# A decoder's second cross-attention: fillers out of TensorE's score units, and GpSimd's row scaling rewritten

## The reference

```
x = x + xattn(layernorm(x), ctx_2048, ...)   # layernorm: (x - mean) / sqrt(var + 1e-5)
q = (x @ Wq + bq) ;  k, v = split(ctx @ Wkv + bkv)      # 16 heads of 16 features
q, k = int8-like rounding per head ;  v rounded per column
attn = softmax(q @ k.T)                                 # all 1024 queries against all 1024 keys
attn = round(attn / (max / 255)) * (max / 255)          # codes 0 .. 255 per row
out  = (attn @ v) @ Wp + bp
x = x + moe(layernorm(x), ...)
```

## Time and profile before

| | us |
|---|---|
| median of 3 runs | 539.23 (538.76 to 540.14) |
| the profiled execution | 539.08 |
| its span in the trace | 537.3 |
| score units: first score product to end of last exponential | 223.12 to 406.2 |
| PE busy | 426.8 (79%) |
| DVE busy | 417.2 (78%) |
| ACT busy | 339.0 (63%) |
| POOL busy | 260.9 (49%) |

### The profile page before, as it was taken

One profiled execution on the slowest core, in us unless ns is written; L12 is line 12 of the kernel. 1 busy time (PEld: TensorE's weight loads), 2 busy tenths in 40 slices (PEclk: granted clock), 3 DMA queues, 4 the chain that ended last, 5 costly groups with the idle time before them and its releaser, 6 DMA issues.

```text
span 537.3 us, 11046 instructions
## 1 busy us (share of the span) xinstructions
PE 426.8 (79%) x3880; PEld 284.3 (53%) x3915; DVE 417.2 (78%) x832; ACT 339.0 (63%) x629; POOL 260.9 (49%) x442
## 2 busy tenths in 40 slices
PE   7988755767988898577787878877878879989884
PEld 3537542445555565234455545554556348777774
DVE  5998899869689776998999999999895843522244
ACT  2663336954579465398999999999994115445440
POOL 5845410006089465304465464654422058888770
PEclk9997897999899998989999999999899999999999
DMA  8850000000005300399999999999995978996548
GB/s 290 233 196 0 0 1 2 0 1 1 1 1 101 58 2 1 41 168 176 163 186 184 188 196 183 185 190 197 180 177 104 312 226 239 238 231 119 83 73 245
DMA packets 169862, 69.46 MB, mean 129 GB/s; under 512 B 142352, under 2 KB 167632, under 8 KB 169808
## 3 DMA queue, kind: packets, MB, share of 16 engines
q1 hardware_dynamic: 162288, 58.53, 53.2%
q0 software_dynamic: 4704, 7.61, 7.5%
q10 hardware_dynamic: 2816, 2.62, 1.7%
HBM read 27.56 MB, written 7.62 MB: 65 GB/s over the span
## 4 chain that ended last, share of the span: by engine, by line
DVE 40%; PE 20%; issue 16%; POOL 9%; ACT 9%; DMA 6%; DVEq 0%; POOLq 0%; ACTq 0%
DVE nm L1849 12%; DVE AT L1664 5%; DMA A<-x_rows,slot_token 4%; ACT A L933 3%; POOL sums L725 3%; DVE XN L1472 3%; PE ps L1430 2%; POOL A L713 2%; PE ps L1212 2%; PE ps L1001 2%; PE ps L1143 1%; POOL b L647 1%; DVE A L407 1%; DVE SC L1505 1%; PE ps L1404 1%
## 5 line engine op out<-in xcount | busy, mean ns | idle before, releaser
L933 ACT ACTIVATE A<-ps,b,sq 128x1024 int16<-128x1024 f32 x128 | 153.3, 1204 | 13.1 <-DVE b L1854 7.4
L1849 DVE TENSOR_REDUCE nm<-ps 128x1 f32<-128x1024 f32 x128 | 151.7, 1211 | 6.9 <-PE ps L1288 3.8
L1288 PE MATMUL ps<-big,ctx_sb 128*128 128x512 bf16 x225 | 71.5, 388 | 33.2 <-ACT A L933 29.7
L647 POOL TENSOR_SCALAR b<-nm,sq 128x1 f32<-128x1 f32 x120 | 31.7, 264 | 93.3 <-DVE nm L1849 70.4
L1359 PEld LDWEIGHTS ps<-VI,A 128*128 128x128 f16 x1024 | 43.5, 97 | 19.9 <-issue 4.0
L1929 DVE TENSOR_TENSOR AT<-AT,ps 128x128 f32<-128x128 f32 x32 | 9.2, 287 | 51.4 <-ACT AT L955 51.3
L713 POOL DMA_INDIRECT A<-x_rows,slot_token x32 | 35.6, 1113 | 25.2 <-DMA x_rows<-ctx_sb 15.7
L1359 PE MATMUL ps<-VI,A 128*128 128x16 f16 x1024 | 44.5, 170 | 0.2
L1288 PEld LDWEIGHTS ps<-big,ctx_sb 128*128 128x128 bf16 x256 | 15.2, 97 | 48.2 <-ACT A L933 38.8
L725 POOL DMA_INDIRECT sums<-XN,slot_token x22 | 35.8, 1628 | 7.9 <-issue 5.2
L540 POOL TENSOR_SCALAR veps<-mv 128x4 f32<-128x4 f32 x8 | 2.6, 322 | 69.7 <-DVE mv L1465 66.8
(11 more groups left out here) (315 smaller groups left out, 1040.4 us busy)
## 6 DMA issues: line engine op xcount, KB each, us to landing
A<-in SPq DMA_DIRECT2D x32, 256.0 KB, 3.6
A<-in SPq DMA_DIRECT2D x32, 128.0 KB, 4.3
A<-in SPq DMA_DIRECT2D x2, 1024.0 KB, 13.4
A<-A SPq DMA_TRANSPOSE x112, 3.4
X<-in SPq DMA_DIRECT2D x2, 512.0 KB, 4.6
big<-in SPq DMA_DIRECT2D x1, 1024.0 KB, 8.8
ctx_sb<-in SPq DMA_DIRECT2D x1, 1024.0 KB, 16.0
sums<-zeros SPq DMA_DIRECT2D x2, 512.0 KB, 5.1
```

The source lines that it names most:

```text
L647: g.tensor_scalar(b5[:, n % 4:n % 4 + 1], nm5[:, n % 4:n % 4 + 1], sq5[:, q, h:h + 1], LN255, ALU.mult, ALU.add).then_inc(S["pbias5_ready" ...
L933: a.activation(Y5[:, n % YB, :], ps[:, 2 * ((n + 1) % 3):2 * ((n + 1) % 3) + 2, :], ACT.Exp, scale=sq5[:, q, h:h + 1], bias=b5[:, n % 4:n ...
L1288: done = T.matmul(ps[:, 2 * ((n + 1) % 3) + c, :], QT5[:, q % 2, h // 2, h % 2, :], KT5[:, h // 2, c * 512:(c + 1) * 512], start=True, sto ...
L1849: v.tensor_reduce(nm5[:, n % 4:n % 4 + 1], ps[:, 2 * ((n + 1) % 3):2 * ((n + 1) % 3) + 2, :].rearrange("p a c -> p (a c)"), AX.X, ALU.max, ...
```

## The change

Two edits. On TensorE the filler branch is no longer taken before the last score unit; after it the eight products per unit stay as they were. On GpSimd the scaling is written as an add and a multiply, (X + (-mean)) * rstd. The negated mean is a new instruction on 128x1 in the same unit, ahead of it, with a semaphore of its own, on which GpSimd waits before it goes on. `APPLIED` lists the 13 scalings in order, to count that semaphore.

```diff
+        nmean = sb("nmean", [P, NT])
...
+        APPLIED = [(kind, t) for kind, t in LN_ORDER[2:] if (kind, t) != ("r", NT - 1)]
...
             def ln_apply(kind, t):

+                i = APPLIED.index((kind, t))
+                g.tensor_scalar(nmean[:, t:t + 1], mv[:, t, 0:1], -1.0, 0.0, ALU.mult, ALU.add).then_inc(S["nmean_ready"], 1)
+                pool.wait_ge(S["nmean_ready"], i + 1)
                 pool.wait_ge(S["rstd_ready"], 8 + NT + ln(kind, t))
-                g.tensor_scalar(XN[:, t, :], X[:, t, :], mv[:, t, 0:1], rstd[:, t:t + 1], ALU.subtract, ALU.mult).then_inc(S["xn_ready"], 1)
+                g.tensor_scalar(XN[:, t, :], X[:, t, :], nmean[:, t:t + 1], rstd[:, t:t + 1], ALU.add, ALU.mult).then_inc(S["xn_ready"], 1)
...
-                elif side == before and not codes and n < U5 + LAG5 - 1:
-                    for c in range(2 if n < U5 else 8):
+                elif U5 <= n < U5 + LAG5 - 1 and side == before:
+                    for c in range(8):
                         T.matmul(ps[:, 6 + q % 2, D:2 * D], identb[:, :], KT5[:, 0, 0:D], start=True, stop=True)
```

More of the change, by code:

```diff
@@ L251, in decoder_kernel @@
         names = """x_loaded x2_loaded w0_loaded bkv_loaded front_step ctx_loaded wp_loaded w_loaded w1_loaded w2_loaded low_loaded rows_ready
-            const_ready pads_ready rstd_e rstd_ready stats_ready aggr_ready xn_ready x_ready tp_psum tp_ready
+            const_ready pads_ready rstd_e nmean_ready rstd_ready stats_ready aggr_ready xn_ready x_ready tp_psum tp_ready
             qkv_psum qkv_ready prod0_ready prod1_ready step1 exp1_ready at_ready proj_psum
```

## The result

The changed kernel takes 540.43 us (median of 22 runs) against 538.72 us of the kernel before (22 runs on the same chip): ratio 1.0043, 95% interval 1.0024 to 1.0061. It is slower, by 1.7 us (the medians) to 2.3 us (the ratio), where 1.9 us of gain were forecast. The profiled execution took 543.72 us (span 541.7, against 537.3); it is one of the longer ones. Over the 22 executions the time mostly goes with TensorE's mean granted clock: 537.92 to 540.35 us in the seven where that is 0.947 to 0.951, 542.23 to 545.47 us in the six where it is 0.924 to 0.927; but one of 0.938 took 545.38.

What follows compares the result with a forecast made beforehand. The prediction took VectorE and ScalarE to set the pace, with TensorE's scores held once a tile by the wait for XN. Scaling -3.5, clock +1.6 and fillers 0 gave -1.9 us: 537.3 us, range 535.0 to 543.2.

Steps and rivals of the forecast that it cites:

- the clock term: TensorE without fillers: opening at low clock for nothing, four later fallen stretches at 0.4 us each, +1.6 us.
- The scaling: GpSimd's scaling as add and multiply ends 0.50 us sooner, seven times where scores wait for XN: -3.5 us.
- rival C: GpSimd: per-row scalars are the slow part, scaling stays 1.24 us plus an extra instruction; 543.0 us, chance 0.17.
- next late: After GpSimd's scaling, VectorE would bound the tile; its 0.82 us idle lets it take 0.50 and hardly more.
- The fillers' own cost: TensorE's filler products run nearly all inside waits, so removing them frees nothing on the path: 0 us.
- The tail: The part after the last exponential was to stay unchanged.
- B: Fast scaling's gain lost to TensorE's clock: some 12 fallen stretches at 0.4 us, +4.8; 540.5 us, chance 0.13.
- D: Scaling lands between, 0.6 to 0.8 us, and the clock takes the gain back: 538.6 to 539.6 us, chance 0.10.
- A: The forecast itself: fast scaling on GpSimd, few fallen stretches on TensorE; 537.3 us (535.4 to 538.3), chance 0.55.

Runs made afterwards that it cites:

- f3: New scaling with all fillers, one code transpose per tile replaced by a 16-column copy, against the kernel before: 536.19 us, ratio 0.9946.
- f4: Kernel before the change with one code transpose per tile replaced by a 16-column copy, as a control: 538.97 us, ratio 0.9993.
- g3: Changed kernel with fillers back in units 8 to 39 and the negated mean made one unit sooner: 536.51 us, ratio 0.9991 to the kernel before.
- h1: Kernel before the change, old scaling, without the fillers of the first eight score units: 539.19 us, ratio 0.9991.
- g1: Changed kernel with fillers back from unit 8 to the end, none in the opening: 535.70 us, ratio 0.9946 to the kernel before.
- e3: Changed kernel with fillers back in units 0 to 39 only: 539.64 us, ratio 0.9998 to the kernel before.
- g2: Changed kernel with fillers back in units 8 to 39 and from 104 on: 538.99 us, ratio 1.0025 to the kernel before.
- e4: Changed kernel with all fillers back but only 16 columns wide instead of 256: 543.36 us, ratio 1.0088 to the kernel before.
- f1: Changed kernel with fillers back in units 0 to 7 only: 540.92 us, ratio 1.0024 to the kernel before.
- f2: Changed kernel with fillers back in units 8 to 39 only: 536.93 us, ratio 0.9956 to the kernel before.
- e1: New scaling with all fillers kept, against the kernel before: 537.51 us, ratio 0.9986.

## Why the prediction was wrong

540.43 us lies inside the range of 535.0 to 543.2, but the change was to gain 1.9 us and costs 1.7 to 2.3. The step that failed is the clock term.

**The scaling: mechanism right, size a little off.** 128x256 with add and multiply took 0.548 us (0.42 forecast; bounds 0.405 and 1.24), the 128x1 0.190 (0.24), the gap 0.10 (0.08). GpSimd is 0.40 us sooner, not 0.50, and a steady tile is 22.22 us, not 22.15. Over the 128 units f3 and f4 differ by 177.76 - 174.95 = 2.8 us (seven times 0.40), and by their ratios 2.5 us, where -3.5 was forecast. Subtract by two per-row scalars had been the slow form: rival C is out. As next late the prediction named VectorE. It has 0.51 us idle in the tile of 22.22 (0.35 forecast), and the 1.50 us of g3 show that XN still held part of that interval; the transposes on SyncE, which the prediction hadn't named, came up beside.

**The fillers' own cost: right.** Tiles at full clock are 22.22 us with and without fillers (f3, and the changed kernel), as long as the codes are in time.

**The clock: this step failed.** It said an opening at low clock for nothing and four later stretches of 3.4 us at 0.4 us each, +1.6 us. It measured +7.0 us in the profiled execution (the tiles of the changed kernel less those of f3, 181.94 - 174.95). The number of stretches was off by a factor of two: of the 44.3 us, 17.1 are the opening's, and the other 27.2 are eight times 3.4, the last of them just behind the units. At 0.4 each that would still have been +3.2. The price was the larger error. The steady tile with one stretch costs 1.39 us more (23.61), the first two tiles together 4.8 (49.24 against 44.44 in f3), the last 0.8; and the last tile of the kernel before had already shown a fall at 0.66 us (21.14 against 20.48 in f4 and 20.51 in h1). The reasoning behind 0.4 looked only at the score pair, 0.61 to 1.01; it left out that the same rows have fp32 side products whose extra 0.9 us stands ahead of the scores in TensorE's queue. "Side products are dense in every tile" was written down as a reason for a high clock; they are also the place where a low clock is paid, and the opening's low clock, free by itself, ran on into the first of them.

The account of the profiled executions, by stretches that add up to the whole: scaling -2.8 (f3 less f4), the old fall in the last tile gone as a cost of its own, -0.7 (f4 less before), falls in the units +7.0, the tail +1.8 (134.05 against 132.27), the start of the first exponential -0.9 (225.71 against 226.60). Sum +4.4, which is 541.7 less 537.3. The median run is only 1.7 us above the median before; if the scaling gives its 2.8 there too, the falls cost it an estimated 4 to 5 us (1.7 + 2.8).

**The tail** was to be unchanged. In the profiled execution it is 1.8 us longer, and the clock falls at its start (407.6 us). That this fall is the cause is not shown: the tail, from the start of the last exponential, took 134.78 us in f4 and 131.3 in g1, and neither has a fall in its first 125 us. It differs by as much between executions without one.

**The rivals.** B, the gain lost to the clock, gave 540.5 us, which is the median to 0.1; it had 0.13. Its mechanism is the one shown, but the match of the number is luck: its working (twelve stretches of 0.4, all tiles alike) isn't what the trace has, which is fewer falls, most of them in the first two tiles, at a higher price, in an execution that took 543.72. The argument against it, that steady tiles with the same wait for XN had kept 1.00, came from a kernel whose fillers were running. The rule of the Trainium skill that spoke against the edit (page "TensorE: Matmul & The Clock Gate", section "Why this matters for your kernels") was on the right side, though gaps of under 1 us were all that stood ahead of the fall at 353.0. Two sums among the rivals are off and change nothing in this: D's terms give 538.6 to 540.0, not 539.6, and A's eight stretches (538.9) lie outside its own 535.4 to 538.3.

**What stays open.** Why one execution falls in a steady tile and another not, and with it what the eight longer executions of e3 and the five of g2 did. With the new scaling the three falls in steady tiles lie in the same place, 11.3 to 11.4 us behind the tile's first exponential, right ahead of the output projection (the changed kernel at 353.0, e4 at 308.0, g2 at 325.3), but e3, f1 and f2 have no such fall from 250 to 370 us. Also the differences between g1 and e1 and between f2 and e3, and what makes the tail's length.

## What to carry to other kernels

Filler products that run inside waits look free to take out, and here their own time was; price them by what the clock does to the most expensive work on that engine, here the fp32 projections, not by what it does to the work that is always there. Keep them where the side work begins after a stretch of light load (units 8 to 39 here), and give them work to do: 256 columns held the clock, 16 held nothing. A kernel without them can also look well in one execution, so compare many. When a pace gets faster by 2%, look at every queue that kept pace before, DMA transposes too.

## What the runs showed of the hardware that I had not expected

- On GpSimd, 128x256 fp32 with two per-row scalars takes 1.24 us as subtract and multiply, 0.548 as add and multiply; with constants 0.405.
- TensorE fell to 1.2 GHz at 353.0 us while it had been busy for 7.63 of the 10.2 us before, without a gap of over 0.84 us. In the kernel before it was busy for 8.14 us of the same part of the tile (340.9 to 351.1) and didn't fall.
- At 1.2 GHz four 128x256 fp32 products take 1.91 us (1.03 at 2.4 GHz), a score pair 1.01 to 1.03 (0.59 to 0.61), eight value products 0.41 (0.35). Of these three the longer ones show more of the factor of two.
- In f2 13.7 us at low clock cost nothing where VectorE set the pace; in the changed kernel one stretch of 3.4 us cost 1.39 where a projection stood ahead of the scores.
